# Both copies of a stack in one transfer, and the expert weights in four transfers on ScalarE's queue

## The reference

```python
qkv = x @ w_qkv.T                       # 2048 tokens, 16 heads of 8 features
scores = q @ k.T / sqrt(8)              # a token sees itself and the 63 before it
ctx = softmax(scores) @ v
x = layernorm(x + ctx @ w_out.T + b_out)
top2, probs = the two best of 8 experts by x @ gate_w + gate_b, softmax of the two
y_e = silu(((x @ w1[e] + b1[e]) * (x @ w2[e] + b2[e])) @ wg[e] + bg[e]) @ w3[e] + b3[e]
x = layernorm(x + sum over the two experts of prob * y_e)
```

## Time and profile before

| | |
|---|---|
| median of 3 runs | 311.36 us (309.72 to 314.98) |
| the profiled execution | 311.95 us |
| its span, first to last instruction | 310.2 us |
| mean granted TensorE clock | 0.939 |
| busy share of the span | PE 77%, DVE 70%, POOL 52%, ACT 50% |
| moved by DMA | 36.50 MB, 118 GB/s over the span |

### The profile page before, as it was taken

One profiled execution on the slowest core, in us unless ns is written; L12 is line 12 of the kernel. 1 busy time (PEld: TensorE's weight loads), 2 busy tenths in 40 slices (PEclk: granted clock), 3 DMA queues, 4 the chain that ended last, 5 costly groups with the idle time before them and its releaser, 6 DMA issues.

```text
span 310.2 us, 7675 instructions
## 1 busy us (share of the span) xinstructions
PE 237.9 (77%) x1791; PEld 174.1 (56%) x1791; DVE 217.2 (70%) x714; ACT 154.1 (50%) x410; POOL 161.0 (52%) x287
## 2 busy tenths in 40 slices
PE   2386579898979998887597878699999999995000
PEld 1155367676757777775355555566766766764000
DVE  6499537888878988886646677677777776774091
ACT  3636537868676968645125633244444334332043
POOL 6654002667666777777643662223464654656151
PEclk9999979999999999999679999999999999999555
DMA  4563425459686979766320112211111111100522
GB/s 119 181 157 91 137 75 143 128 149 273 195 249 189 281 203 268 181 202 240 113 60 3 36 53 68 78 37 51 42 56 32 51 40 45 48 18 7 201 104 101
DMA packets 33988, 36.50 MB, mean 118 GB/s; under 512 B 4972, under 2 KB 30062, under 8 KB 33824
## 3 DMA queue, kind: packets, MB, share of 16 engines
q1 hardware_dynamic: 30864, 29.69, 33.5%
q0 software_dynamic: 2336, 4.37, 4.3%
q10 hardware_dynamic: 752, 2.03, 2.0%
HBM read 25.48 MB, written 11.05 MB: 118 GB/s over the span
## 4 chain that ended last, share of the span: by engine, by line
PE 47%; DVE 14%; SPq 12%; issue 12%; DMA 8%; POOL 3%; ACT 2%; DVEq 0%; ACTq 0%; POOLq 0%
PE bank L1578 9%; PE bank L1550 8%; PE bank L1541 6%; SPq L409 5%; PE bank L1393 3%; DMA k_stack<-k_scratch 3%; PE bank L1573 2%; PE bank L1397 2%; PE bank L1566 2%; PE bank L1412 2%; DMA expert_out<-probs,tile_x 2%; DVE top L954 2%; SPq L422 2%; DVE shift L964 2%; DMA w_up<-expert_out 2%
## 5 line engine op out<-in xcount | busy, mean ns | idle before, releaser
L713 POOL DMA_INDIRECT expert_out<-probs,tile_x x39 | 40.3, 1034 | 58.2 <-DVE probs L1272 56.2
L813 ACT ACTIVATE probs<-bank 128x512 f32<-128x512 f32 x64 | 34.8, 592 | 20.0 <-PE bank L1397 19.6
L664 POOL DMA_INDIRECT routed<-rows,place x32 | 33.2, 1037 | 21.4 <-issue 16.5
L1578 PE MATMUL bank<-w_up,x_unit 128*128 x78 | 41.7, 617 | 0.0
L1550 PE MATMUL bank<-w_gate,x_all 128*128 x156 | 40.4, 382 | 0.5 <-DVE v_aug L1263 0.5
L1277 DVE TENSOR_TENSOR w_rows<-bank,b_up 128x512 f32<-128x512 f32 x39 | 26.8, 688 | 18.5 <-PE bank L1578 18.3
L964 DVE TENSOR_TENSOR shift<-top,delta_block 64x256 fp32r<-64x256 f32 x64 | 30.1, 471 | 11.9 <-PE bank L1397 9.5
L1541 PEld LDWEIGHTS bank<-w_down,xT 128*128 128x128 f32 x156 | 20.4, 190 | 31.2 <-issue 31.2
L888 ACT COPY x_unit<-bank 128x128 f32<-128x128 f32 x39 | 10.3, 264 | 55.3 <-PE bank L1558 55.1
L1393 PE MATMUL bank<-q_stack,k_stack 128*128 128x256 f32 x128 | 28.4, 305 | 10.9 <-issue 7.4
L954 DVE TENSOR_REDUCE top<-bank 128x4 f32<-128x384 f32 x64 | 33.5, 549 | 2.0 <-PE bank L1376 1.3
(11 more groups left out here) (177 smaller groups left out, 538.2 us busy)
## 6 DMA issues: line engine op xcount, KB each, us to landing
k_stack<-k_scratch SPq DMA_DIRECT2D x28, 160.0 KB, 3.2
q_stack<-q_scratch SPq DMA_DIRECT2D x62, 64.0 KB, 2.5
tile_x<-routed SPq DMA_DIRECT2D x39, 65.0 KB, 1.8
k_scratch<-k_parts SPq DMA_DIRECT2D x7, 320.0 KB
q_scratch<-q_parts SPq DMA_DIRECT2D x8, 256.0 KB
w_up<-in_L_ffn_w_dram SPq DMA_DIRECT2D x16, 128.0 KB
w_gate<-in_L_ffn_wg_dram SPq DMA_DIRECT2D x8, 256.0 KB
b_up<-in_L_ffn_b_dram SPq DMA_DIRECT2D x2, 1024.0 KB
```

What stands on the lines that cost most here:

```text
L664: eng.indirect_dma_start(routed, bass.IndirectOffsetOnAxis(ap=place[i][:, k:k + 1], axis=0), rows[i][:, k, :], None, bounds_check=SPARE + ...
L713: eng.indirect_dma_start(expert_out, bass.IndirectOffsetOnAxis(ap=tile_x[i][:, P:P + 1].bitcast(I32), axis=0), y[i][:, :], None, bounds_ch ...
L813: eng.activation(probs[t[1] % 2][a][:, 512 * h:512 * h + 512], t_bank[h][:, :], ACT.Exp).then_inc(probs_ready, 1)
L1578: eng.matmul(up_bank[:, :], tile_xT[n[1] % 2][:, :], of_expert(w_up, e[0])).then_inc(up_made, 1)
```

## The change

Stack transfers: the source pattern gets a leading dimension of step 0 and count 2, so that one transfer writes both copies: 4 transfers for queries (`Q_PARTS`), 2 for keys (`K_PARTS`), 96 for a unit on the semaphore (`STACKED`). The layout of `q_stack` is changed so that a partition's four groups lie side by side (index `hh` ahead of the group), and line 1394 reads it accordingly. For unit 0 POOL issues one query transfer instead of two, ACT two key transfers instead of four.

Expert weights: SP's 32 transfers are gone; ACT issues two transfers (w1, w2) at the end of slot 2 and two (wg, w3) at the end of slot 3, each with all experts.

POOL: the bias is added in four instructions of four steps each, behind a wait for the second unit's keys; the second stack is zeroed in slot -2, ahead of POOL's wait for its own stack transfer.

```diff
-        POOL_PARTS = 2
+        Q_PARTS, K_PARTS = 4, 2
+        POOL_PARTS = 1
+        STACKED = 16 * (Q_PARTS + K_PARTS)
-        def stack_queries(eng, i, part):
-            hh, dup = part // 2, part % 2
+        def stack_queries(eng, i, hh):
+            held = q_scratch[i].rearrange("w (d h g) n -> h (w d) (g n)", d=HD, h=4)[hh]
             return eng.dma_start(
-                q_stack[i][64 * dup + hh:64 * dup + hh + 61:4, :, hh, :].bitcast(F32),
-                q_scratch[i].rearrange("w (d h g) n -> h (w d) g n", d=HD, h=4)[hh])
+                q_stack[i][hh:hh + 125:4, hh, :, :].rearrange("p g n -> p (g n)").bitcast(F32),
+                bass.AP(held.tensor, held.offset, [[0, 2], *held.ap]))
...
-        def stack_keys(eng, i, part):
-            return eng.dma_start(k_stack[i][32 * part:32 * part + 32, :, :].bitcast(F32),
-                                 k_scratch[i][part // 2].rearrange("(r g) n -> r g n", g=4))
+        def stack_keys(eng, i, w):
+            held = k_scratch[i][w].rearrange("(r g) n -> r (g n)", g=4)
+            return eng.dma_start(k_stack[i][64 * w:64 * w + 64, :, :].rearrange("p g n -> p (g n)").bitcast(F32),
+                                 bass.AP(held.tensor, held.offset, [[0, 2], *held.ap]))
...
-                    for part in range(8):
-                        if s != -2 or part < 8 - POOL_PARTS:
+                    for part in range(Q_PARTS):
+                        if s != -2 or part < Q_PARTS - POOL_PARTS:
                             stack_queries(eng, i, part).then_inc(stacked[i], 16)
                     if s != -2:
                         eng.wait_ge(k_out, ucount(u, 16, 16))
-                        for part in range(4):
+                        for part in range(K_PARTS):
                             stack_keys(eng, i, part).then_inc(stacked[i], 16)
...
-                if s is None:
-                    e = t[0] * 4 + (t[1] - 4)
-                    for c, w in enumerate((w1, w2)):
-                        eng.dma_start(w_up[:, bass.ds(e, 1), c, :],
-                                      w[bass.ds(e, 1)].rearrange("e h f -> h e f")).then_inc(experts_loaded, 16)
-                    for held, w in ((w_gate, wg), (w_down, w3)):
-                        eng.dma_start(held[:, bass.ds(e, 1), :, :].rearrange("p e c n -> p (e c) n"),
-                                      w[bass.ds(e, 1)].rearrange("e (c p) n -> p (e c) n", p=P)).then_inc(experts_loaded, 16)
...
-                if s == -1:
-                    eng.memset(q_stack[1][:, :, :, :].bitcast(F32), 0.0).then_inc(zeros_ready[1], 1)
                 if s == 1:
                     eng.wait_ge(loaded, 16 * 4)
-                    eng.tensor_tensor(x_all[:, :, :], x_all[:, :, :], bo[:, :].unsqueeze(1).to_broadcast([P, STEPS, P]),
-                                      ALU.add).then_inc(xb_ready, 1)
+                    eng.wait_ge(k_lo, 2)
+                    for q in range(4):
+                        held = x_all[:, 4 * q:4 * q + 4, :]
+                        eng.tensor_tensor(held, held, bo[:, :].unsqueeze(1).to_broadcast([P, 4, P]), ALU.add).then_inc(xb_ready, 1)
...
                     for part in range(Q_PARTS - POOL_PARTS, Q_PARTS):
                         stack_queries(eng, 0, part).then_inc(first_stacked, 16)
+                    eng.memset(q_stack[1][:, :, :, :].bitcast(F32), 0.0).then_inc(zeros_ready[1], 1)
                     eng.wait_ge(first_stacked, 16 * POOL_PARTS)
...
+                if s == 2:
+                    for c, w in enumerate((w1, w2)):
+                        eng.dma_start(w_up[:, :, c, :], w.rearrange("e h f -> h e f")).then_inc(experts_loaded, 16)
                 if has(s, 3, STEPS + 2):
                     gap_of_two(later(t, -3))
+                if s == 3:
+                    for held, w in ((w_gate, wg), (w_down, w3)):
+                        eng.dma_start(held[:, :, :, :].rearrange("p e c n -> p (e c) n"),
+                                      w.rearrange("e (c p) n -> p (e c) n", p=P)).then_inc(experts_loaded, 16)
...
-                wait(eng, stacked[i], pcount(u, 192))
+                wait(eng, stacked[i], pcount(u, STACKED))
...
-                                   q_stack[i][:, grp, :, QT * w:QT * w + QT], start=(l == 0), stop=False,
+                                   q_stack[i][:, :, grp, QT * w:QT * w + QT], start=(l == 0), stop=False,
```

More of the change, by code:

```diff
@@ L452, in slot @@
                     i = u[1] % 2
-                    wait_apart(eng, wait_value, const_ready, stacked[i], pcount(later(u, -2), 192))
+                    wait_apart(eng, wait_value, const_ready, stacked[i], pcount(later(u, -2), STACKED))
                     wait(eng, q_hi, ucount(u, 1, 1))
@@ L683, in slot @@
                     eng.wait_ge(zeros_ready[0], 1)
-                    for part in range(8 - POOL_PARTS, 8):
+                    for part in range(Q_PARTS - POOL_PARTS, Q_PARTS):
                         stack_queries(eng, 0, part).then_inc(first_stacked, 16)
+                    eng.memset(q_stack[1][:, :, :, :].bitcast(F32), 0.0).then_inc(zeros_ready[1], 1)
                     eng.wait_ge(first_stacked, 16 * POOL_PARTS)
@@ L735, in _ @@
             eng.wait_ge(early_chain, EARLY_LINKS)
-            eng.wait_ge(experts_loaded, 16 * (4 * E + 4))
+            eng.wait_ge(experts_loaded, 16 * (4 + 4))
             run_end(piece, tile_slot)
@@ L989, in residual @@
                 if is_step(t, 0):
-                    eng.wait_ge(xb_ready, 1)
+                    eng.wait_ge(xb_ready, 4)
                 wait(eng, y_made, count(t, 1, 1))
```

## The result

The changed kernel takes 470.58 us (median of 4 runs, 469.21 to 472.16), the kernel before 311.81 us on the same occasion (309.72 to 314.98). The ratio is 1.513, with a 95% interval of 1.503 to 1.523. The profiled execution took 472.16 us and has a span of 470.4 us and a mean granted clock of 0.80. A ratio leaves out every run that is more than 1.5% above the fastest of its kernel, so it can differ from the ratio of the medians beside it.

The account below looks back on a forecast made before the run. First-stage stack transfers on two engines would bind: 37 + 7 x 32.1 = 262 us for unit 7, 273 with weights, plus 177.6 behind it = 451, 452 as profiled execution, less 2 caught up: 450 us, range 400 to 510.

Parts of the forecast that it names:

- The engines: Stack transfers with two copies outermost get only two of the 16 DMA engines; chance 0.85.
- The rate of an engine: Each DMA engine moving the stacks' 4 to 5 KB rows carries 25.4 GB/s, with 17.8 as the bad end.
- The circle: First stage: PE makes the next unit's keys behind this unit's first score matmuls, so late stacks delay it; period 32.1 us.
- First transfer to PE's start: In each unit's period: 2.3 us fixed latency, 23.2 us moving the stack, 1.5 us other traffic.
- the term for other traffic on the two engines: Key store ahead in SP's queue and part of the scatters pass through the stacks' two engines: 1.5 us a unit.
- The first stack: Unit 0's stack lands at 37 us, POOL's quarter of the queries perhaps going on other engines.
- The weights: Expert weights on ACT's queue meet the stacks of units 2 and 3 on the two engines, adding 11 us.
- two gaps of 7.4 us: Times in two unit periods without stack movement (5.1 + 2.3 us), taking up some 7 us of the weights' 18.4.
- The additions and the zeroing: POOL's split additions and earlier zeroing bring nothing; the additions' 3 us lie in PE's wait for the stack.
- Behind unit 7: From PE's first matmul on unit 7 to the end: 177.6 us, less an estimated 2 us for trailing work caught up.
- Rival 1: Stack transfers use 16 engines; saved issue gains about 7 us, DVE's hold-up 3 us more: 302 us; chance 0.09.
- Rival 2: 16 engines are used, but the weight burst delays stacks 2 and 3 by 4 us each: 310 us; chance 0.06.

## Why the prediction was right, step by step

The forecast was 450 us, with a range of 400 to 510; measured were 470.6.

*The engines* (two of sixteen): right, by a share of 0.12 at 51 GB/s and the series of counts. The count of two did it in a kernel without any repeated row. The Trainium skill ("DMA: Bandwidth & Descriptors", "Rules for kernel authors") states that an outermost count under 16 confines a transfer to at most that many engines. The runs agree: shares of 0.12, 0.25 and 0.51 for counts of 2, 4 and 8.

*The rate of an engine*, 25.4 GB/s from the earlier trace rows: right, 25.5 in most of the single microseconds in which only a pair is at work. The microseconds at 31 GB/s for the pair were not foreseen.

*The circle*: right in kind; it was worth 34 us in the changed kernel. Its first part was put at 5.1 us, measured from the chain are 4.6 to 6.3, on average 5.7 (40.89 to 45.52, up to 254.47 to 260.09). That is 4 us in seven units. One thing that fits: PE comes out of the long waits at a granted clock of 0.50, the lower level (252 to 253 us above), and its first matmul pair takes 0.77 us where the earlier trace rows have 0.50 and 0.48. It is not shown to be the cause: unit 0's pair takes the same 0.77 us at a granted clock of 1.00 (41 to 42 us).

*First transfer to PE's start*, put at 27.0 us (2.3 + 23.2 + 1.5): mis-sized. The seven were 26.7, 37.4, 29.5, 27.4, 29.5, 28.6 and 32.1 us. Without the second, which has the weight burst, they are 29.0 on average; the term for other traffic on the two engines should have been 3.5 and not 1.5. What it is most likely made of is SP's queue: query stores and token loads, which wait behind one stack on these two engines, go through ahead of the next. I had counted only the key store and a part of the scatters; no run separates them. The 32.1 of the last unit stand out. SP issues the first two bias loads of 1 MB each (b1 and b2) behind just this stack, from 265.26 on, and from 287 us to 291 us, right before PE's start at 292.20, the DMA share is 1.01 to 1.12. That these loads hold the stack up fits, but was not tested. The kernel with a count of two, which has the same loads there, has a long last wait too (18.3 us against 15.9).

*The first stack*, put at 37: came at 40.9. POOL's query transfer did not go beside the others: it landed after 13.5 us, and from 18 to 25 us, with it under way, the share of all engines is 0.12 to 0.13, which is one pair.

*The weights*, put at 11 us: the unit that meets them took 37.4 us where the others took 29.0, so 8.4, and the two kernels with and without the burst are 5.2 us apart in time. The 11 were 18.4 less "some 7" for two gaps of 7.4 us, of which only half was taken off without a reason. I had called ACT's four issues hidden at 0.5 us each. They were not so short:

```profile
87.70 9.27 ACTq L868 DMA_DIRECT2D w_gate<-in_L_ffn_wg_dram  x1
...
97.20 19.71 ACTq L868 DMA_DIRECT2D w_down<-in_L_ffn_w_dram  x1
117.20 1.09 ACT L807 ACTIVATE probs<-bank 128x512 f32<-128x512 f32 x2 [20.04 <-PE bank L1398]
```

The last issue held ACT from 97.2 to 116.9 us. PE had started on unit 2 at 115.12, so most of that lay in the wait, as said.

*The additions and the zeroing*, put at nothing: nothing in the runs speaks against it, but no run has them alone. The misses up to unit 7 are 3.9 (first stack) + 4 (circle) + 14 (seven times 2.0) - 2.6 (weights) = 19.3 us; 273 + 19 = 292, which is where unit 7 started.

*Behind unit 7*, put at 177.6 less 2 us for work that has caught up: that credit did not come, the stretch took 178.2 us. This is the other 2.6 us of the 22 by which the profiled execution (472.16) is over the forecast. So the mechanism was right; of the sum, the traffic beside the stacks was the term that was sized too small by most.

*Rival 1* (16 engines, a gain of 10 us): its premise is false. Of its price, the part for units from 2 on was too: the kernel with half the issues brought nothing there. The step that failed in it was to count 4 us for each unit in which the circle binds without asking which wait comes next. Its 3 us for the additions did not show either, as the kernel with the copies apart and the weights on SP is at the time of before. Its 4 us for unit 1 stay untested. *Rival 2's* mechanism is real: with all engines at work the burst delays units 2 and 3, and with the burst the kernel is slower, 317.5 us against 312.0.

## What to carry to other kernels

When a transfer's pattern is rewritten, look at what is now outermost, not only at the number of transfers and their bytes: the count there set how many of the 16 DMA engines the transfer got, and the "merged" transfer with 2 outermost ran on two of them. Before trading for fewer issues, ask what PE would wait for next; half the issues from unit 2 on brought nothing here, while moving the producer of the next transfer out of the wait for the current one brought 1.7% by reordering alone.

## What was not expected

A DMA issue can hold its engine for a long time: ACT's issue of w3 took 19.71 us and that of wg 9.27 us in the changed kernel, where two issues of weights took 0.91 us together on SP; with the copies apart the w3 issue still took 6.54 us. On SP, the issues of b1 and b2 took 5.0 and 12.7 us. I read this as a queue that is full because two busy engines hold up everything in it; no run shows how full a queue is.

What stays open: why the kernel with a count of two and the copies apart is 14 us faster than the changed one, which has the same two engines and the same bytes. The two differ in the repeated reading, in the size of the transfers and in POOL's share, which concerns unit 0 only (PE starts on it at 39.02 against 40.89). No run separates these. One trace in the middle of it: from SP's first query transfer to PE's start on unit 6 it takes 25.9 us (214.15 to 240.10), against 28.6 in the changed kernel.
